# Joining a rewritten projection, held mamba weights and sums spread by products with the half-tile mamba kernel

## The chip, the cores and the metric

The kernel runs on one core of one Trainium2 chip. The metric is the device time of one execution in microseconds (us), as the median of several runs. The engines of a core work in parallel, each through its own list of instructions, and wait for one another by semaphores: PE (TensorE) multiplies matrices, DVE (VectorE), ACT (ScalarE) and POOL (GpSimd) work on elements, and SP (SyncE) here only issues transfers. POOL issues transfers too, on a queue of its own.

## The reference

One layer over x of 2 batches x 2048 tokens x 256 channels (T = 4096 rows), all in float32:

```python
xn = _layernorm(x)
x = x + mamba(xn, ...) + ffn(xn, ...)
# mamba: inner width 512, state 16, convolution over 4 taps, low rank 64
x_and_res = xn @ W_in; xs = silu(conv(x_and_res[:, :512]))
dt = softplus((xs @ W_x)[:, :64] @ W_dt + b_dt)
h_t = exp(dt*A) * h_(t-1) + dt*B*xs ; y = C.h + xs*D ; out = (y * silu(res)) @ W_out
# ffn: 16 heads of 16, then 8 experts of width 1024, one per token
hn = _layernorm(xn, g, b); q, k, v = hn @ wq + bq, hn @ wk + bk, hn @ wv + bv
x1 = xn + softmax(q k / 4) v @ wo + bo
hn2 = _layernorm(x1, g2, b2); idx = argmax(hn2 @ gate_w + gate_b)
result = x1 + relu(hn2 @ w1[idx] + b1[idx]) @ w2[idx] + b2[idx]
```

## The kernel before

The work runs in five stages, one after the other. Each stage is a block in which every engine has its own list, and the next block begins when all of them have ended. Rows are taken in 8 chunks of 512 tokens (`BANK`), four tiles of 128 rows each (`TG`).

**Projection** (`phase_project`, lines 112 to 430). A chunk of x is loaded by POOL (L201) into one of two buffers `X[s]`. DVE takes its moments (`variance`: bn_stats L379, bn_aggr L383, L385), ACT the root (L337), DVE refines it in five steps on tiny tiles (`rstd_steps`, L105 to L109) and normalises the rows in place (L392): that is xn, which SP stores to `xn_d` (L243). The same is done a second time on xn and gives `HN`, which POOL multiplies by g (L207) and adds b to (L211). PE turns both over (L301), ACT copies the turned xn out (L346) and DVE the turned HN (L422). PE then multiplies it for queries and keys (four products of 2 x 512 columns, L310) and for values (L316), with the value bias as one more product per tile (L318). ACT evicts each query or key tile twice (L353 in float32, L356 rounded to fp32r) and DVE forms the rest of the rounding (`QP[n][:, 1, :]`, L429), and SP stores both parts (L261). ACT copies the value tiles (L361) into one of two buffers, and SP stores each of four tiles per chunk (L266). The chunks run as a hardware loop over pairs; the normalisation of chunk c + 1 is laid between the query and key tiles of chunk c. POOL's order within chunk c is the scaling of chunk c + 1, then the load of chunk c + 2, which waits until PE has turned chunk c.

**Mamba** (`phase_mamba`). SP first loads ten weights (L879 to L888), among them `conv_w` copied to all partitions, and then the turned rows of the first two chunks (L891). DVE waits for all ten and makes the convolution weights of the four taps, eight products of 128x512 (`WC`, L1309). PE's first convolution (L1129) waits for them. The scans that follow are untouched by the change.

**Attention** (`phase_attention`). 32 items of one head group and one query block. PE makes the scores twice, once for their maxima (L642, reduced by DVE at L736) and once for the exponentials (L655, ACT at L714), and then the products with the values (L665). The maxima of an item reach the query tile as 16 small transfers (L574), for which the first L655 of the next item waits. At eight places, one in about four items, POOL loads three tiles of 512 KB for later (L623: xn, x and the output of mamba), adds the bias bo to the first (L625) and the mamba output to the second (L627).

**Routing** (`phase_route`). For each chunk SP loads the unscaled attention output into `OT` (L1438, four transfers) and the inverse row sums, each row copied to the 16 partitions of its head, into `SM` (L1446, four more). DVE multiplies them (`scale`, L1588), PE projects (L1513, into two buffers in turn), DVE adds the rows (L1592), takes moments and normalises (L1608), PE turns the rows over and makes gate logits (L1524, L1535), DVE chooses the expert and counts slots, POOL adds the base (L1490) and scatters the row numbers (L1495), SP stores `hn_d` and `base_d` (L1467, L1470). SP issues the loads of chunk c + 2 at the start of its turn c, behind the stores of chunk c - 1.

**Experts** (`phase_experts`). 23 tiles of 256 rows; untouched.

## Time and profile before

| what | us |
|---|---|
| median of 3 runs | 3401.77 (3387.27 to 3415.67) |
| the profiled execution | 3394.42 |
| span of its trace | 3392.8 |
| projection, from 0 to | 217.5 |
| mamba, to | 1320 |
| attention, to | 2865 |
| routing, to | 3040.3 |
| experts, to | 3392.8 |

The trace is of one execution. Its span leaves 1.6 us of the profiled time outside, and that execution is 7.4 us below the median.
### The profile page before, as it was taken

What the parts mean: (1) busy time and instruction counts of PE and PEld (TensorE: products, weight loads), DVE (VectorE), ACT (ScalarE), POOL (GpSimd) and SP (SyncE); (2) the same over time, 40 slices, a digit from 0 to 9 for tenths busy, and PEclk for the clock granted to TensorE, in tenths of its full rate; (3) what the DMA queues carried; (4) which work ended last, traced back from release to release, by engine and by line L of the source; (5) the groups of instructions that cost most, each with busy time, mean ns of one, the idle gap of its engine ahead of it and who ended that gap; (6) DMA issues with size and microseconds to landing.
All of it is one profiled execution on the core that took longest, in us unless ns stands there. A gap on an engine that the chain in (4) does not pass through costs nothing. (4 is left out here: it accounts for less than half of the span.)

```text
span 3392.8 us, 42834 instructions
## 1 busy us (share of the span) xinstructions
PE 2898.4 (85%) x12668; PEld 1374.2 (41%) x12668; DVE 2594.8 (76%) x3764; ACT 1708.7 (50%) x2088; POOL 930.6 (27%) x527
## 2 busy tenths in 40 slices
PE   5768799898998775999989999998999996539998
PEld 3333343343443332433333333333333332428887
DVE  5525999999999995988889888898989992542222
ACT  2324655655655631366667666676767776101110
POOL 2203565565565565000000000000000000234443
PEclk8879999999999887699999999999999998669999
DMA  4542122212121224655444555445554410336663
GB/s 150 170 141 81 64 75 81 69 75 80 69 84 66 69 68 55 78 86 68 68 76 62 85 68 80 74 60 79 67 86 60 63 21 27 112 106 198 200 204 120
DMA packets 218021, 300.80 MB, mean 89 GB/s; under 512 B 117906, under 2 KB 162476, under 8 KB 203346
## 3 DMA queue, kind: packets, MB, share of 16 engines
q1 hardware_dynamic: 205298, 268.27, 36.1%
q0 software_dynamic: 12512, 29.82, 2.9%
q8 instruction: 120, 1.97, 0.3%
q14 instruction: 91, 0.75, 0.1%
HBM read 245.37 MB, written 57.60 MB: 89 GB/s over the span
## 5 line engine op out<-in xcount | busy, mean ns | idle before, releaser
L736 DVE TENSOR_REDUCE attn_mx<-attn_pX 128x1 f32<-128x512 f32 x2048 | 1271.9, 683 | 187.8 <-PE attn_pX L642 185.9
L714 ACT ACTIVATE attn_pr<-attn_pS 128x1024 f32<-128x1024 f32 x1024 | 992.6, 1022 | 529.8 <-PE attn_pS L655 529.3
L642 PE MATMUL attn_pX<-attn_ks,attn_qs 48*128 48x512 f32 x2048 | 757.0, 497 | 75.0 <-DMA attn_vs<-v_d 25.2
L1198 PE MATMUL mamba_pY<-mamba_g,mamba_ident 128*128 128x512 f32 x1024 | 516.1, 651 | 139.9 <-DVE mamba_g L1351 139.7
L1331 DVE TENSOR_TENSOR_SCAN mamba_h<-mamba_pA,mamba_hs,mamba_db 128x512 f32<-128x512 f32 x512 | 616.7, 1263 | 12.9 <-ACT mamba_pA L1046 12.6
L642 PEld LDWEIGHTS attn_pX<-attn_ks,attn_qs 48*128 48x128 f32 x2048 | 308.3, 193 | 779.7 <-DVE attn_mx L736 715.5
L981 POOL TENSOR_TENSOR mamba_db<-mamba_bq,mamba_u 128x2048 f32<-128x2048 f32 x128 | 580.3, 4534 | 75.3 <-DVE mamba_u L1287 75.0
L665 PE MATMUL attn_pO<-attn_pr,attn_vs 128*17 128x512 f32 x4096 | 558.7, 618 | 0.4 <-ACT attn_pr L714 0.4
L1046 ACT ACTIVATE mamba_pA<-mamba_dt,mamba_an 128x512 f32<-128x512 f32 x512 | 352.7, 692 | 389.9 <-DVE mamba_h L1331 389.6
L655 PE MATMUL attn_pS<-attn_qs,attn_ks 50*128 50x512 f32 x2048 | 474.4, 418 | 52.9 <-DMA attn_qs<-attn_mt 32.7
L1198 PEld LDWEIGHTS mamba_pY<-mamba_g,mamba_ident 128*128 128x128 f32 x1024 | 200.9, 205 | 444.7 <-DVE mamba_g L1351 228.8
L1351 DVE TENSOR_TENSOR mamba_g<-mamba_h,mamba_bq 128x2048 f32<-128x2048 f32 x128 | 293.7, 2294 | 6.5
L655 PEld LDWEIGHTS attn_pS<-attn_qs,attn_ks 50*128 50x128 f32 x2048 | 258.4, 194 | 92.1 <-issue 55.1
L623 POOL DMA_DIRECT2D rows_xn<-xn_d x8 | 6.1, 767 | 1021.8 <-PE attn_pO L665 1021.8
L1129 PE MATMUL mamba_pP<-mamba_xt,mamba_wc 128*128 128x512 f32 x512 | 230.7, 596 | 24.2 <-DVE mamba_an L1312 24.2
L1875 DVE TENSOR_SCALAR exp_hm<-exp_pH,exp_b 128x256 f32<-128x256 f32 x46 | 22.3, 484 | 234.7 <-PE exp_pH L1813 234.7
L1839 ACT ACTIVATE exp_hm<-exp_pH,exp_b 128x256 f32<-128x256 f32 x46 | 21.8, 474 | 320.3 <-PE exp_pH L1813 320.3
L1813 PE MATMUL exp_pH<-exp_xt,exp_w 128*128 128x256 f32 x736 | 165.1, 383 | 1.1 <-DVE exp_xt L1854 1.1
L1826 PE MATMUL exp_pY<-exp_w,exp_hm 128*128 128x256 f32 x736 | 162.7, 379 | 0.0
L1129 PEld LDWEIGHTS mamba_pP<-mamba_xt,mamba_wc 128*128 128x128 f32 x512 | 97.7, 191 | 148.6 <-issue 148.6
L1813 PEld LDWEIGHTS exp_pH<-exp_xt,exp_w 128*128 128x128 f32 x736 | 141.4, 192 | 21.1 <-DVE exp_xt L1854 1.5
L1826 PEld LDWEIGHTS exp_pY<-exp_w,exp_hm 128*128 128x128 f32 x736 | 138.1, 190 | 17.9
(185 smaller groups left out, 1926.7 us busy)
## 6 DMA issues: line engine op xcount, KB each, us to landing
mamba_bq<-bc_d SPq DMA_DIRECT2D x64, 1024.0 KB, 4.6
attn_ks<-parts_d SPq DMA_DIRECT2D x192, 256.0 KB, 9.1
exp_w<-in_w SPq DMA_DIRECT2D x46, 1024.0 KB, 5.5
attn_vs<-v_d SPq DMA_DIRECT2D x32, 544.0 KB, 15.6
parts_d<-proj_qp SPq DMA_DIRECT2D x32, 512.0 KB, 2.9
attn_qs<-parts_d SPq DMA_DIRECT2D x192, 64.0 KB, 8.2
attn_qs<-attn_mt SPq DMA_DIRECT2D x512, 1.0 KB
oraw_d<-attn_oe SPq DMA_DIRECT2D x32, 256.0 KB, 2.1
```

Source lines behind the costliest of these rows:

```text
L642: pe.matmul(pX[bank(s, n)][:, :], QS[slot][rows, pair, qt * P:(qt + 1) * P], KS[slot][rows, pair, part * BANK:(part + 1) * BANK], start=Tr ...
L655: mm = pe.matmul(pS[pair][:, h, :], KS[slot][rows, pair, kt * P:(kt + 1) * P], QS[slot][rows, pair, :], start=True, stop=True)
L665: mm = pe.matmul(pO[32 * h:32 * h + VW, :], VS[s][:, kt, h, :], PR[2 * (kt % 2) + h // 2][:, h % 2, :], start=(kt == 0), stop=(kt == KT - 1))
L714: act.activation(PR[2 * (kt % 2) + pair][:, :, :], pS[pair][:, :, :], ACT.Exp, scale=HD ** -0.5).then_inc(p_sb, 1)
L736: dve.tensor_reduce(MX[:, col:col + 1], pX[bank(s, n)][:, :], AX.X, ALU.max).then_inc(x_max, 1)
L981: pool.tensor_tensor(DB[k % 2][:, :, :], BQ[q % 2][:, 0, :, :], U[s][:, j, :].unsqueeze(1).to_broadcast([P, QN, BANK]), ALU.mult).then_inc ...
L1046: act.activation(pA[n % 2][:, :], DT[s][:, j, :], ACT.Exp, scale=AN[:, j, q * QN + n:q * QN + n + 1]).then_inc(da_done, 1)
L1129: mm = pe.matmul(bank(par, place)[:, :], WC[:, k, a, w], XT[sx][:, k, a:a + BANK], start=(k == 0 and a == 0), stop=(k == KC - 1 and a == T ...
L1198: mm = pe.matmul(pY[j][:, :], ident[:, :], G[k % 2][:, n, :], start=False, stop=(q == NQ - 1 and n == QN - 1))
L1331: dve.tensor_tensor_scan(H[k % 2][:, n, :], pA[n % 2][:, :], DB[k % 2][:, n, :], HS[:, j, q * QN + n:q * QN + n + 1], ALU.mult, ALU.add).t ...
L1813: mm = pe.matmul(pH[n][:, f % 2, :], W1[s][:, k, f * P:(f + 1) * P], XT[s][:, k, :], start=(k == 0), stop=(k == KC - 1))
L1826: mm = pe.matmul(pY[s][:, t, :], HM[s][:, f, t * P:(t + 1) * P], W2[s][:, f, :], start=(f == 0), stop=(f == KF - 1))
```

## The change

The half-tile mamba kernel takes over three edits.

1. `phase_project` is written anew, with the eight chunks unrolled. Three buffers for x in place of two; the normalisation runs two chunks ahead in place of one; four buffers for the query and key parts in place of two; whole-chunk buffers for the values. xn is no longer stored to memory (`xn_d` is gone); its means and inverse roots are kept in `mv1` and `rstd1` instead. The product that added the value bias is gone; POOL adds it to a chunk of 128x1024 elements (`value_bias`).
2. The weights of mamba are loaded in the projection stage into tiles that are held through both stages, and POOL makes the tap products there, two in each of chunks 2 to 5. The mamba stage begins with the loads of its rows.
3. In attention POOL loads two tiles in place of three at each of the eight places and makes xn from x by a subtraction and a multiplication. In routing the inverse sums come as rows of 16 heads (`INV`, 7 small loads and the late ones), and PE spreads each to its 16 partitions by a product with a matrix of zeros and ones (`SEL`), two products of 512 columns per chunk; DVE multiplies from PSUM. `pA` is one buffer in place of two, and the loads of `OT` run three chunks ahead in place of two.

```diff
@@ phase_project, POOL
+                def value_bias(c):
+                    pool.wait_ge(v_sb, TG * (c + 1))
+                    v = VS[c % 2][:, :, :, 0:HD]
+                    pool.tensor_tensor(v, v, BV[:, :].rearrange("p (h d) -> p h d", d=HD).unsqueeze(1)
+                                       .to_broadcast([P, TG, HEADS, HD]), ALU.add).then_inc(v_done, 1)
+
+                for c in range(RX):
+                    load_x(c)
...
+                scale(0)
+                scale(1)
+                def tap(n):
+                    k, a = divmod(n, TAPS)
+                    a = TAPS - 1 - a
+                    pool.tensor_tensor(WC[:, k, a, :], WC[:, k, 0, :], CW[:, a, :], ALU.mult).then_inc(wc_done, 1)
+
+                for c in range(NCH):
+                    if c + RX < NCH:
+                        load_x(c + RX)
+                    value_bias(c)
+                    if c == 2:
+                        pool.wait_ge(mamba_ld, 16 * (len(mamba_w) + 1))
+                    if 2 <= c < 2 + KC * TAPS // 2:
+                        tap(2 * (c - 2))
+                        tap(2 * (c - 2) + 1)
+                    if c + 2 < NCH:
+                        scale(c + 2)
@@ SP
+                sp.dma_start(WC[:, :, 0, :], mamba_in[0]).then_inc(mamba_ld, 16)
+                for dst, src in zip(mamba_w[1:], mamba_in[1:]):
+                    sp.dma_start(dst, src).then_inc(mamba_ld, 16)
...
+                for c in range(NCH):
+                    store_turned(c)
+                    store_part(c, 0)
+                    store_part(c, 1)
+                    store_part(c, 2)
+                    store_part(c, 3)
+                    store_values(c)
+                sp.wait_ge(wc_done, KC * TAPS)
@@ PE
+                pe.wait_ge(id_ready, 2)
+                turn(0)
+                pe.wait_ge(w_in, 16 * 8)
+                for c in range(NCH):
+                    queries_keys(c)
+                    if c + 1 < NCH:
+                        turn(c + 1)
+                    values(c)
@@ ACT
+                for c in range(NCH):
+                    split(c, 0)
+                    split(c, 1)
+                    if c + 2 < NCH:
+                        root(c + 2, 0)
+                    split(c, 2)
+                    split(c, 3)
+                    if c + 1 < NCH:
+                        copy_turned(c + 1)
+                    if c + 2 < NCH:
+                        root(c + 2, 1)
+                    copy_values(c)
@@ DVE
+                for c in range(2):
+                    first_norm(c)
+                    second_norm(c)
+                    scaled_rows(c)
+                copy_turned(0)
+                for c in range(NCH):
+                    if c + 2 < NCH:
+                        first_norm(c + 2)
+                    low(c, 0)
+                    low(c, 1)
+                    if c + 2 < NCH:
+                        second_norm(c + 2)
+                    low(c, 2)
+                    low(c, 3)
+                    if c + 1 < NCH:
+                        copy_turned(c + 1)
+                    if c + 2 < NCH:
+                        scaled_rows(c + 2)
@@ phase_attention, POOL
-                    for dst, src in ((XN[c], xn_d), (XB[c], x), (MOB, mo_d)):
+                    for dst, src in ((XB[c], x), (MOB, mo_d)):
...
+                    pool.tensor_tensor(XN[c][:, :, :], XB[c][:, :, :], mean, ALU.subtract).then_inc(x_done, 1)
+                    pool.wait_ge(x_done, 3 * c + 1)
+                    pool.tensor_tensor(XN[c][:, :, :], XN[c][:, :, :], rstd, ALU.mult).then_inc(x_done, 1)
@@ phase_mamba
-                dve.wait_ge(w_ld, 16 * 10)
-                for a in range(TAPS - 1, -1, -1):
-                    for k in range(KC):
-                        ins = dve.tensor_tensor(WC[:, k, a, :], WC[:, k, 0, :], DB[0][:, a, :], ALU.mult)
-                ins.then_inc(ready_s, 1)
@@ phase_route, SP
+                for g in range(GB):
+                    load_inverses(0, g)
+                load_o(0)
+                for b in range(1, batches):
+                    for g in range(GB - (b == batches - 1)):
+                        load_inverses(b, g)
                 load_o(1)
-                load_r(1)
+                load_o(2)
@@ PE
+                def spread(c):
+                    if c >= 1:
+                        pe.wait_ge(scaled, c)
...
+                    for k in range(KC):
+                        mm = pe.matmul(pS[:, k, :], SEL[:, k, :], INV[:, c, :], start=True, stop=True)
+                    mm.then_inc(s_ps, 1)
...
                 for c in range(NCH):
                     if c + 1 < NCH:
                         project(c + 1)
+                    if c + 2 < NCH:
+                        spread(c + 2)
                     turn(c)
@@ DVE
-                    dve.tensor_tensor(OT[c][:, :, :], OT[c][:, :, :], SM[c][:, :, :], ALU.mult).then_inc(scaled, 1)
+                    dve.wait_ge(s_ps, c + 1)
+                    dve.tensor_tensor(OT[c][:, :, :], pS[:, :, :], OT[c][:, :, :], ALU.mult).then_inc(scaled, 1)
```

## Rows read from the trace of the kernel before

**Rows 1.** Busy time by stage: from:to, length, each engine (instructions), PEclk, DMA share, GB/s
```profile
0.00:217.50 217.50, 141.68 (x448) 76.32 (x448) 103.31 (x340) 64.05 (x129) 49.51 (x30) 0.88 0.51 161
...
1320.00:2865.00 1545.00, 1414.83 (x8194) 536.80 (x8192) 1301.82 (x2180) 1008.75 (x1058) 87.21 (x54) 0.94 0.48 68
2865.00:3040.30 175.30, 76.41 (x352) 65.02 (x352) 90.14 (x301) 18.38 (x41) 52.39 (x47) 0.65 0.35 99
```

**Rows 2.** The same view of seven projection periods and of seven routing periods
```profile
26.20:196.20 170.00, 124.06 (x393) 66.33 (x393) 88.01 (x284) 53.27 (x108) 42.36 (x20) 0.86 0.53 167
2888.60:3007.50 118.90, 59.95 (x284) 50.87 (x284) 69.27 (x227) 14.43 (x35) 37.14 (x27) 0.70 0.37 112
```

**Rows 3.** Who waited for whom in the projection: total us, times, longest
```profile
POOL proj_hn L207 <- DVE proj_hn L392: 141.8, 8, 19.9
DVE proj_stats L379 <- DMA proj_x<-in_x: 54.0, 7, 8.3
ACT proj_vs L361 <- DMA v_d<-proj_vs: 50.4, 16, 5.9
```

**Rows 4.** Timeline, projection: start, length, engine, line, operation, [idle before <-releaser]
```profile
20.86 2.34 POOL L211 TENSOR_TENSOR proj_hn<-proj_hn,proj_b 128x1024 f32<-128x1024 f32 x1
...
26.87 1.38 DVE L392 TENSOR_SCALAR proj_x<-proj_x,proj_meanvar,proj_rstd 128x256 f32<-128x256 f32 x4
...
31.34 0.69 DVE L429 TENSOR_TENSOR proj_qp<-proj_qf,proj_qp 128x512 fp32r<-128x512 f32 x1 [0.91 <-ACT proj_qp L356]
...
187.75 2.72 POOL L207 TENSOR_TENSOR proj_hn<-proj_hn,proj_g 128x1024 f32<-128x1024 f32 x1 [18.17 <-DVE proj_hn L392]
...
189.18 1.84 DVE L429 TENSOR_TENSOR proj_qp<-proj_qf,proj_qp 128x512 fp32r<-128x512 f32 x1 [0.91 <-ACT proj_qp L356]
...
209.77 0.69 PE L318 MATMUL proj_pV<-proj_bv,proj_one 1*128 1x256 f32 x2
```

**Rows 5.** Timeline, start of the mamba stage
```profile
217.55 0.39 SPq L879 DMA_DIRECT2D mamba_wc<-in_w_in  x1
...
229.67 4.91 DVE L1309 TENSOR_TENSOR mamba_wc<-mamba_wc,mamba_db 128x512 f32<-128x512 f32 x8 [11.46 <-DMA mamba_ds<-in_d_skip]
...
234.68 29.88 PE L1129 MATMUL mamba_pP<-mamba_xt,mamba_wc 128*128 128x512 f32 x64 [24.22 <-DVE mamba_an L1312]
```

**Rows 6.** Timeline of attention at one of the eight places
```profile
1768.59 0.77 POOL L623 DMA_DIRECT2D rows_xn<-xn_d  x1 [125.88 <-PE attn_pO L665]
...
1774.48 0.51 PE L655 MATMUL attn_pS<-attn_qs,attn_ks 50*128 50x512 f32 x2 [3.37 <-DMA attn_qs<-attn_mt]
```

**Rows 7.** Busy time in tens of us, attention, around two of the eight places
```profile
1760.00:1770.00 10.00, 9.72 (x59) 3.81 (x63) 9.39 (x16) 7.11 (x8) 1.41 (x2) 1.00 0.01 1
1770.00:1780.00 10.00, 4.88 (x26) 1.17 (x18) 4.80 (x8) 3.17 (x4) 3.97 (x4) 0.75 0.58 186
1780.00:1790.00 10.00, 9.50 (x50) 3.89 (x52) 6.26 (x10) 5.82 (x6) 1.53 (x1) 0.74 1.00 132
...
1910.00:1920.00 10.00, 8.15 (x43) 2.82 (x44) 6.50 (x11) 5.50 (x7) 4.73 (x4) 0.75 0.74 217
1920.00:1930.00 10.00, 9.75 (x56) 4.20 (x56) 8.59 (x14) 6.70 (x7) 1.29 (x1) 0.91 1.07 117
```

**Rows 8.** Instructions of line 736, attention: duration ns min/median/max
```profile
L736 DVE TENSOR_REDUCE attn_mx<-attn_pX x1992: 649/681/694, 1379.7 to 2814.1; 128x1 f32<-128x512 f32 x200
```

**Rows 9.** Waits, transfers (KB each) and one window of the routing stage
```profile
DVE route_ot L1588 <- DMA route_sm<-rs_d: 51.0, 6, 18.9
...
route_ot<-oraw_d SPq DMA_DIRECT2D x32, 128.0 KB
...
2874.00:2876.00 2.00, 0.00 (x0) 0.00 (x0) 0.00 (x0) 0.00 (x0) 0.00 (x0) 0.50 0.26 97
```

**Rows 10.** Timeline of the routing stage
```profile
2899.49 1.22 DVE L1592 TENSOR_TENSOR rows_xn<-route_pA,rows_xn 128x1024 f32<-128x1024 f32 x1 [3.77 <-PE route_pA L1513]
...
2917.69 4.23 DVE L1608 TENSOR_SCALAR route_hn<-rows_xn,route_meanvar,route_rstd 128x256 f32<-128x256 f32 x4
```

More of the change, by code:

```diff
@@ L161, in phase_project @@
         xn_done = m.sem("xn_done")
-        xn_out = [m.sem(f"xn_out{s}") for s in range(2)]
+        mamba_ld = m.sem("mamba_ld")
+        wc_done = m.sem("wc_done")
         hn_raw = m.sem("hn_raw")
@@ L363, in _, with root, copy_turned @@
-                chunks(act, body)
+                def root(c, n):
+                    act.wait_ge(var_ready, 2 * c + n + 1)
+                    act.activation(ROOT[:, :], V[:, :], ACT.Sqrt).then_inc(root_ready, 1)
+                def copy_turned(c):
+                    if c >= 2:
+                        act.wait_ge(xnT_out[c % 2], sum(pads(a) for a in range(c % 2, c, 2)))
+                    for k in range(KC):
+                        act.wait_ge(x_turned, KC * c + k + 1)
+                        act.copy(TX[c % 2][:, k, :], pT[k][:, :]).then_inc(x_sb, 1)
@@ new lines, in copy_values @@
+                def copy_values(c):
+                    if c >= 2:
+                        act.wait_ge(v_out[c % 2], 16 * GB * (c // 2))
+                    for t in range(TG):
+                        act.wait_ge(v_ps, TG * c + t + 1)
+                        act.copy(VS[c % 2][:, t, :, 0:HD], pV[t % 2][:, 0:C].rearrange("p (h d) -> p h d", d=HD)
+                                 ).then_inc(v_sb, 1)
+                for c in range(2):
+                    for n in range(2):
+                        root(c, n)
@@ L791, in phase_mamba @@
     NQ = N // QN
-    TAPS = conv_w.shape[0]
+    TAPS = WC.shape[2]
     PAD = TAPS - 1
@@ L1398, in phase_route @@
         CMP = m.sb("cmp", [P, NTL, NE])
-        pA = [m.ps(f"pA{n}", [P, TG, C]) for n in range(2)]
+        pA = m.ps("pA", [P, TG, C])
+        pS = m.ps("pS", [P, KC, BANK])
         pT = [m.ps(f"pT{n}", [P, 2, KC, P]) for n in range(2)]
```

491 lines of the change are left out of this document (229 added, 262 removed).

## The prediction

> **What bounds the kernel now.** I read the busy time by stage first [rows 1]. Attention is full: PE works 1414.8 of 1545 us. Projection and routing are not. In the projection no engine is busy for more than 142 of 217.5 us, and the DMA engines are at 0.51; in routing PE has 76 of 175 us and DVE 90. These two stages wait on chains, and the change works on them. Experts and the scans of mamba keep their instructions, so I take their time as it is.
>
> Then the waits of the projection [rows 3]. DVE waits 54.0 us in 7 of 8 chunks for the load of x, ACT 50.4 us for a value buffer to be stored, and POOL 141.8 us for rows to scale. That is one loop: POOL loads chunk c + 2 only after it has scaled chunk c + 1, so the load comes late, so DVE's moments, so the rows to scale. Seven periods, from the first chunk's first query product at 26.2 to the last chunk's, take 170 us, 24.3 each, in which DVE is busy 88.0 us (12.6 a period), PE 124.1 and POOL 42.4 [rows 2].
>
> Routing I read in the same way [rows 2, 9, 10]. Seven periods take 118.9 us, 17.0 each, though the first, to the next L1592 at 2899.5, takes 10.9. DVE waits 51.0 us for the `SM` loads. While only the `OT` and `SM` loads run, the DMA share is 0.26 at 97 GB/s. Eight loads of 128 KB (1.05 MB) thus take 10.7 us of every period.
>
> **Projection.** The new order removes the loop: x is loaded three ahead and the moments are two chunks ahead, so none of the three waits of [rows 3] is left to last. What bounds it next is DVE with POOL. DVE keeps its instructions, 12.6 us a chunk. POOL, which had two products of 2.34 us alone [rows 4], gets `value_bias` of the same size, 7.0 us in all, and in chunks 2 to 5 two taps of a quarter of that size each way, near 1.2 us each: 9.4 us.
>
> The rows show that these two don't simply lie side by side. L429 takes 1.84 us when it starts at 189.18 under L207, which runs from 187.75 for 2.72 us; the difference from its usual 0.69 is about the time that POOL still had [rows 4]. In routing four L1608 take 4.23 us under POOL [rows 10]. They have the elements of L392, four of which cost 1.38 us [rows 4], so 2.8 us were lost. L736, with one input in PSUM, never takes over 694 ns [rows 8], whatever POOL does. So DVE instructions that read SBUF wait for a POOL instruction under way, and others pass. About 4.9 of DVE's 12.6 us are such others (bn_stats, bn_aggr, copies from PSUM). The period is bounded by 14.4 us (12.6 and 1.8 for handing over between PE, ACT and DVE) if nothing collides, and by 12.6 + 7.0 = 19.6, or 22.0 with taps, if all does. I lay one period out: the scaling product runs beside the next moments, but then holds the first `low`, and `value_bias` holds the last one. That gives 17.8 us, and 20 with taps, nearer the upper bound, since both groups of `low` come just when POOL has something ready.
>
> The Trainium skill (SBUF — State Buffer, Who interferes with whom) says the same more sharply, and it speaks against moving work to POOL: the pair is an exclusive lock that one instruction holds for its whole length, `tensor_tensor` contends when both inputs lie in SBUF, and `tensor_reduce` never does. By that rule, the trace agrees (1.84 us against 0.69).
>
> PE is no bound: its 124.1 us in seven periods are 17.7 each at a clock of 0.86, and the bias products (0.69 us per tile in [rows 4]) fall away, some 2.8 us. The transfers are none either: 0.53 of 24.3 us is 12.9 us a chunk, of 4.1 MB, less an eighth for xn.
>
> The start gets longer. DVE now does two chunks before the first copy for PE, and the second one's normalisation waits for POOL's product that ends at 23.2 [rows 4]. I put the first query product at 32 (before: 26.2). Then two periods of 17.8, four of 20, chunk 6 without new rows at 12.4 (PE's products and turning at the upper clock), and chunk 7 at 10.3: 32 + 35.6 + 80 + 12.4 + 10.3 = 170.3. The tail was 7 us (last value product 210.5, stage end 217.5); it gets `value_bias` in the chain, so 9. The stage ends at 179 in place of 217.5: **38 us saved**. With 14.4 us throughout it would end near 150 (67 saved), with 19.6 and 22.0 near 191 (26 saved). The 3 MB of weights and taps lie in the first 20 us of the queue, where stores have nothing to do yet; if they delayed the third x by some us, it is inside these bounds.
>
> **Mamba start.** From the first load at 217.55 to PE's first convolution there are 17.1 us: 12 for weights to land, 4.9 for the taps [rows 5]. What remains is the load of the first rows, 515 KB, for which I take 4 us (the twelve of before moved some 3.5 MB; half a MB is under 2, and as much for issue and landing). **13 us saved**, with 11 and 14 as ends. PE idles before in both cases, so its first convolutions are at the lower clock in both.
>
> **Attention.** At each of eight places 1.5 MB of loads from POOL fall on the 16 small transfers of the maxima. PE waits (3.37 us in [rows 6]), and its clock then goes from 1.00 to 0.50 for a while. PE issued 76 products in the 20 us after 1770, where undisturbed it issues 60 in ten, and 99 after 1910 [rows 7]: 7 and 3.5 us lost, so some 5 a place and 42 in all. One third of the bytes goes. I take a little less than a third of it, **12 us saved**; below is 0 (the small transfers still end behind the other two loads), above 30 (the clock isn't lost at most places). The two added POOL products, 4.7 us a place, hide behind L736, which doesn't wait for POOL [rows 8]. If that cover were gone, they would cost 8 x 4.7 = 38 us.
>
> **Routing.** The `SM` loads go, half of the 10.7 us. 17.0 - 5.3 = 11.7 is then what the transfers need. DVE is busy 69.3/7 = 9.9 us a period; the fastest period seen is 10.9 [rows 10]. PE gets two products of 512 columns per chunk, 1.7 us at the upper clock and 3.4 at the lower, beside DVE's normalising, but now behind one `pA`. I take 12.3: 118.9 - 86.1 = **33 us saved**. The bounds are 10.9 (43 saved) and 15 (14 saved), where PE at its lower clock sets it: 60 us of PE in seven periods at 0.70 [rows 2] make 12 each at 0.50, and 3.4 more. The first `SM` gives way to seven small loads in front of `scale(0)` and a product; I take that start as even.
>
> **The sum.** 38 + 13 + 12 + 33 = 96. The profiled execution of before took 3394.4, so 3298. It is 7 us below the median of 3401.8, which would give 3306; I say 3300.
>
> **Rivals.**
> - *POOL doesn't hold DVE in the new order* (periods of 14.4): for it, only some of the products of the rows are held; against it, `low` and the scaling are both due once a chunk. 29 us more saved: 3271.
> - *Routing isn't helped*, since PE at the lower clock, with one `pA` and the spreading in its chain, takes 15.4 to 16 us a period: for it PEclk 0.65 in the stage [rows 1]. 26 us less saved: 3326.
> - *Attention keeps its clock* at most places, since a shorter stall might not cost it: 20 more saved, 3280. Against it, the smaller disturbance at 1910 lost the clock too (0.75, [rows 7]).
> - *No change or slower.* One mechanism could do it: in the projection POOL's list (load, bias, taps, scaling) becomes the loop that everything waits for, each link in turn, as it was with the loads. It decides when the projection's mean period passes 33 us (24.3 now, and 58 us of gains elsewhere over seven periods). POOL, DVE and PE's longest shares, one after the other, are 9.4 + 12.6 + 10 = 32. So even a full chain gives about 3395, no change. Three chunks of buffers speak against it.
> - *The change doesn't do what it says*: the taps or weights end the projection late, since SP waits for them. Taps are done in chunk 5, two periods before the end, so I give it nothing of its own.
>
> **How the numbers follow.** Forecast as summed 0.57 (its own range 3280 to 3318), POOL harmless 0.14, attention keeps its clock 0.10, routing not helped 0.14, chain in the projection 0.05. From 3255 (the first and third together) to 3340 (routing not helped and 19.6 us periods) leaves out 2 in 10. About 1%, 34 us, is what a measurement of this kernel can tell from no change. Every case but the last is faster by more; half of the last and a little of the routing case with other losses fall inside: faster 0.94, same 0.04, slower 0.02.
>
> **What would show it.** Right: no wait of DVE for x; L429 and the normalising over their lone times under POOL; PE's first convolution 4 us after the stage's first load; waits for the maxima at eight places, shorter; no wait of `scale` for loads in routing. Wrong: projection periods under 15 or over 22 us; L736 over 694 ns; routing periods at 15.

## The result and the profile after

| | kernel before | changed kernel |
|---|---|---|
| median | 3396.34 us (3387.27 to 3415.67, 4 runs) | 3313.62 us (3312.34 to 3314.77, 4 runs) |
| ratio, with its 95% interval | 1 | 0.9749 (0.9704 to 0.9794) |
| span of the profiled execution | 3392.8 | 3310.9 |
| projection | 217.5 | 174.3 |
| mamba, first load to first convolution | 17.1 | 3.7 |
| mamba, the rest | 1089.0 | 1088.2 |
| attention | 1543.4 | 1551.6 |
| routing | 173.3 | 140.1 |
| experts | 352.5 | 353.0 |

The changed kernel is faster by 2.5%, 82 us. Stages are read from the first instruction of one to the first of the next (so the end of mamba before is 1323.6 and that of attention 2867.0, where the rows above had the rounder 1320 and 2865). They say where the 82 us come from: 43.2 from the projection, 13.5 from the start of mamba, 33.2 from routing, 1 from mamba's rest. Attention gave 8.2 back.

The stages of the changed kernel (the view of busy time by stretch; columns as in [rows 1]: from:to, length, PE, PE loads, DVE, ACT, POOL, granted clock, DMA share, GB/s). The last two rows answer to [rows 2]: the seven periods of the projection and of routing.

```profile
0.00:174.30 174.30, 113.58 (x384) 69.58 (x384) 135.45 (x339) 63.45 (x129) 74.60 (x46) 0.92 0.72 195
...
1266.20:2817.80 1551.60, 1421.73 (x8192) 538.15 (x8192) 1300.53 (x2180) 1008.34 (x1058) 111.57 (x63) 0.93 0.47 65
2817.80:2957.90 140.10, 95.70 (x384) 72.02 (x384) 95.19 (x301) 17.89 (x41) 52.36 (x51) 0.68 0.50 93
```

```profile
31.00:152.80 121.80, 99.08 (x337) 60.68 (x338) 112.16 (x258) 53.58 (x109) 61.13 (x33) 0.92 0.73 196
2841.20:2925.40 84.20, 75.30 (x312) 56.50 (x312) 74.32 (x227) 13.52 (x34) 36.11 (x27) 0.78 0.64 113
```

Seven executions with this same projection ended it between 172.4 and 176.4 us, so differences of 4 us between two of them mean nothing. DVE is now busy for 112.2 of 121.8 us, where it was 88.0 of 170. It has fewer instructions there than in [rows 2] (258 for 284, since two chunks are normalised before the first period) and takes more time for them: it waits inside its instructions. In routing DVE is busy for 74.3 of 84.2 us. Two of the seven periods take 10.8 and 10.9 us, the other five 12.5 or 12.6. Each of those five holds one tiny DVE instruction that took 2.90 to 2.95 us for its usual 0.17 or 0.19, beside POOL's addition of the rows (L1506); the two short periods hold none:

```profile
2884.20 2.90 DVE L1653 TENSOR_TENSOR route_oh<-route_wtt,route_mw 128x32 f32<-128x32 f32 x1
2884.69 2.35 POOL L1506 TENSOR_TENSOR rows_xb<-rows_xb,rows_xn 128x1024 f32<-128x1024 f32 x1
```

So DVE, held by POOL once a period, bounds the five: in four of them, read one by one, it is busy for 11.7 or 11.8 of 12.5 us, and the period is the same whether the clock is 0.73 or 0.86. PE isn't far behind (10.8 to 12.2 us busy), and no run shows what the period would be without the hold. In the kernel before, the same instruction (L1621) took 0.19 us in all eight chunks, and three others were held in seven periods (two L1608 of 3.26 us, one L107 of 2.94).

The timeline of the projection (start, length, engine, line, operation; lines between are left out):

```profile
68.82 3.43 DVE L437 TENSOR_TENSOR proj_qp<-proj_qf,proj_qp 128x512 fp32r<-128x512 f32 x2
...
68.96 2.74 POOL L198 TENSOR_TENSOR proj_hn<-proj_hn,proj_b 128x1024 f32<-128x1024 f32 x1
...
135.82 5.25 DVE L411 TENSOR_SCALAR proj_hn<-proj_x,proj_meanvar,proj_rstd 128x256 f32<-128x256 f32 x4
135.87 2.17 POOL L204 TENSOR_TENSOR proj_vs<-proj_vs,proj_bv 128x1024 f32<-128x1024 f32 x1 [8.26 <-ACT proj_vs L365]
138.00 2.60 POOL L216 TENSOR_TENSOR held_wc<-held_wc,proj_cw 128x512 f32<-128x512 f32 x2
```

The pair of low parts (L437) takes 3.43 us under the scaling (L198), where two take 1.29 alone. The normalising of chunk 7 (L411) takes 5.25 for 1.38 us, and ends at 141.1, half a us after bias and taps.

The start of mamba, which answers to [rows 5]:

```profile
174.32 0.89 SPq L903 DMA_DIRECT2D mamba_xt<-xnT_d  x2
...
177.99 29.50 PE L1140 MATMUL mamba_pP<-mamba_xt,held_wc 128*128 128x512 f32 x64 [14.60 <-DMA mamba_xt<-xnT_d]
```

One of the eight places in attention, which answers to [rows 6]: SP issues the 16 small transfers of the maxima, one every 0.68 us, POOL issues its two loads before SP is through, and PE waits.

```profile
2128.59 10.88 SPq L600 DMA_DIRECT2D attn_qs<-attn_mt  x16
...
2137.86 0.78 POOL L649 DMA_DIRECT2D rows_xb<-in_x  x1 [130.96 <-PE attn_pO L697]
2138.63 0.76 POOL L649 DMA_DIRECT2D attn_mob<-mo_d  x1
...
2143.03 0.50 PE L687 MATMUL attn_pS<-attn_qs,attn_ks 50*128 50x512 f32 x2 [2.63 <-DMA attn_qs<-attn_mt]
```

The last small transfer is issued from 2138.84 to 2139.5, just after the issue of the second load has begun. In the whole stage PE's wait for them is what it was (32.7 us before; waits: total, times, longest):

```profile
PE attn_pS L687 <- DMA attn_qs<-attn_mt: 32.5, 26, 4.5
```

The clock is lost at the places as it was ([rows 7]; here around 1992):

```profile
1992.20:2002.20 10.00, 6.51 (x34) 2.16 (x32) 4.91 (x8) 4.40 (x5) 5.29 (x4) 0.76 0.33 106
2002.20:2012.20 10.00, 9.93 (x54) 4.18 (x51) 7.58 (x13) 5.88 (x7) 4.69 (x2) 0.73 0.94 137
2012.20:2022.20 10.00, 9.65 (x62) 3.39 (x58) 9.39 (x16) 7.64 (x8) 0.00 (x0) 1.00 1.06 117
```

In routing DVE itself no longer waits for loads ([rows 9]); what it waits for is the first spreading, for which PE in turn waits 15.5 us until the inverse sums have landed, and three of the projections:

```profile
DVE route_ot L1620 <- PE route_pS L1531: 15.1, 1, 15.1
...
DVE rows_xn L1624 <- PE route_pA L1540: 8.9, 3, 3.8
```

### The profile page after: what moved, and what is told of

Same layout as the page of the kernel before. It is cut to its first block and busy times, and to the rows that moved or that the text cites. A ratio compares the mean times of both kernels' runs of the same rounds, so it can differ in the third digit from the quotient of the medians.

```text
span 3310.9 us, 42346 instructions
## 1 busy us (share of the span) xinstructions
PE 2899.2 (88%) x12636; PEld 1377.2 (42%) x12636; DVE 2625.1 (79%) x3755; ACT 1707.4 (52%) x2088; POOL 979.1 (30%) x554
## 5 line engine op out<-in xcount | busy, mean ns | idle before, releaser
L768 DVE TENSOR_REDUCE attn_mx<-attn_pX 128x1 f32<-128x512 f32 x2048 | 1271.3, 683 | 197.6 <-PE attn_pX L674 197.5
L1057 ACT ACTIVATE mamba_pA<-mamba_dt,held_an 128x512 f32<-128x512 f32 x512 | 352.6, 692 | 390.2 <-DVE mamba_h L1335 389.8
L687 PE MATMUL attn_pS<-attn_qs,attn_ks 50*128 50x512 f32 x2048 | 478.2, 421 | 52.8 <-DMA attn_qs<-attn_mt 32.5
L1140 PE MATMUL mamba_pP<-mamba_xt,held_wc 128*128 128x512 f32 x512 | 230.3, 596 | 14.6 <-DMA mamba_xt<-xnT_d 14.6
L1140 PEld LDWEIGHTS mamba_pP<-mamba_xt,held_wc 128*128 128x128 f32 x512 | 97.5, 191 | 139.0 <-issue 124.0
## 6 DMA issues: line engine op xcount, KB each, us to landing
attn_vs<-v_d SPq DMA_DIRECT2D x32, 544.0 KB, 15.7
```

What stands on the lines that cost most here:

```text
L687: mm = pe.matmul(pS[pair][:, h, :], KS[slot][rows, pair, kt * P:(kt + 1) * P], QS[slot][rows, pair, :], start=True, stop=True)
L768: dve.tensor_reduce(MX[:, col:col + 1], pX[bank(s, n)][:, :], AX.X, ALU.max).then_inc(x_max, 1)
L1057: act.activation(pA[n % 2][:, :], DT[s][:, j, :], ACT.Exp, scale=AN[:, j, q * QN + n:q * QN + n + 1]).then_inc(da_done, 1)
L1140: mm = pe.matmul(bank(par, place)[:, :], WC[:, k, a, w], XT[sx][:, k, a:a + BANK], start=(k == 0 and a == 0), stop=(k == KC - 1 and a == T ...
```

## The experiments

Each run has a short name, given behind "Measured" and used in the table of attention. "Unchanged" is the changed kernel as it came. A second comparison of it ("again") had a profiled execution with a span of 3306.0 us, and a median of 3319.73 (ratio 0.9779, 0.9756 to 0.9802), so two medians of one kernel lie 6 us apart. The medians of the kernel before, measured anew in each comparison, lie between 3394.0 and 3403.8; a ratio compares kernels of different comparisons better than a median does. A stage's time is that of one profiled execution.

### Attention: other moments for POOL's loads

First, the loads half an item earlier:

```diff
-                    pool.wait_ge(pv_done, (3 * c + 2) * KT)
+                    pool.wait_ge(pv_done, (3 * c + 2) * KT - KT // 2)
```

> The changed kernel, with POOL's two loads at each of the eight places in attention issued half an item earlier (about 22 us), clear of the 16 small transfers of the maxima. Only the order moves, nothing is left out. Theory A (the stall comes from the small transfers that are issued last and lie behind 1 MB of POOL's load; a third fewer bytes doesn't end it, another time does): PE waits no longer for attn_qs at the places, the granted clock stays at 1.00 there, and attention falls from 1551.6 us by 5 a place, to about 1512. Rival B (the stall belongs to the maxima's own transfers, which SP needs 10.9 us to issue, and happens with or without the load): attention stays within 5 us of 1551. Rival C (the loads lower the clock wherever they fall): the low clock moves with the loads, no gain.

Measured ("shift"): median 3307.85 us (3296.99 to 3328.05), ratio 0.972 (0.969 to 0.975). In its profile attention took 1563.9 us. That execution was the slowest of the four, 20 us over the median, and the median lies below the two of the unchanged kernel, so 1563.9 overstates what the edit cost. Its attention fits none of the theories, but its places show what happened:

```profile
1418.20 1.89 POOL L655 TENSOR_TENSOR rows_xn<-rows_xn,norm_rstd 128x1024 f32<-128x1024 f32 x1
1418.20 1.92 DVE L778 TENSOR_TENSOR attn_ms<-attn_mn,attn_ms 128x16 fp32r<-128x16 f32 x1
```

```profile
1416.00:1426.00 10.00, 7.89 (x38) 3.35 (x39) 7.84 (x14) 3.88 (x4) 8.46 (x4) 0.74 0.01 1
1426.00:1436.00 10.00, 10.00 (x46) 3.78 (x42) 6.70 (x12) 5.41 (x6) 0.00 (x0) 0.57 0.01 3
```

The products moved with the loads, onto the small DVE operations that split the maxima. L778, 0.17 us long, took 1.92, exactly to the end of POOL's product, the next maxima came late, and PE waited 2.03 us for them. The clock fell with no transfer under way (DMA share 0.01). PE's wait for the maxima at the places is gone (11.9 us in the whole stage for 32.5), as theory A says of the loads. What is lost by the clock at the places is as much as with the loads (27 us for 22, in the table below), but now beside the products.

Then the products were put back, behind a second wait:

```diff
                     pool.wait_ge(x_in, 32 * (c + 1))
+                    pool.wait_ge(pv_done, (3 * c + 2) * KT)
```

> The changed kernel, with POOL's two loads at each of the eight places in attention issued half an item earlier (as in the run before), but POOL's four products held back to their old moment. The first shift put the products onto DVE's small operations that split the maxima (L775 to L785), whose rows grew from 0.17 to 1.92 us. Theory A (the small transfers issued last lie behind POOL's load; and the products, where they are, cost nothing): with the loads away and the products back, PE doesn't wait for attn_qs at the places, the granted clock stays at 1.00 there, and attention falls to 1505 to 1525 us (1543 to 1554 in four executions of the unchanged code). Rival B (the transfers of the maxima come too late by themselves): attention stays at 1543 to 1554 with the wait for attn_qs at 30 us.

Measured ("shift2"): median 3293.24 us (3290.58 to 3299.0), ratio 0.9676 (0.9659 to 0.9693): 20 to 26 us below the changed kernel's two medians, 25 to 35 us by the ratios. Attention took 1527.0 us, just above the range of theory A. Around the place that was shown above the clock is kept:

```profile
1960.65 0.78 POOL L649 DMA_DIRECT2D rows_xb<-in_x  x1 [105.87 <-PE attn_pO L698]
...
1982.48 1.89 POOL L654 TENSOR_TENSOR rows_xn<-rows_xb,norm_meanvar 128x1024 f32<-128x1024 f32 x1 [20.30 <-PE attn_pO L698]
```

```profile
1980.80:1990.80 10.00, 9.62 (x61) 3.77 (x63) 9.20 (x15) 7.64 (x9) 8.15 (x4) 1.00 0.11 32
1990.80:2000.80 10.00, 9.67 (x62) 3.57 (x60) 9.35 (x16) 7.46 (x8) 0.34 (x1) 1.00 1.02 127
```

```profile
PE attn_pS L688 <- DMA attn_qs<-attn_mt: 13.6, 24, 4.5
```

POOL works for 8.15 of the ten us from 1980.8 and DVE and PE lose nothing, so the four products, at this moment, cost nothing that shows. PE issues 123 products in 20 us, where the changed kernel had 88. The wait fell from 32.5 to 13.6 us. The stall was thus made by the loads lying in front of the last small transfers.

### Attention: the third load back

```diff
-                    for dst, src in ((XB[c], x), (MOB, mo_d)):
+                    for dst, src in ((XN[c], x), (XB[c], x), (MOB, mo_d)):
```

> The changed kernel, with a third load of 512 KB at each of the eight places (x into the tile of xn, which the subtraction then overwrites), so the transfers are those of the kernel before and the two added products stay. Theory A (the stall's length doesn't follow the bytes, once the small transfers are behind any load): attention within 6 us of 1551.6. My recorded theory (5 us a place, a third of it by the third load): about 12 us longer, 1564.

Measured ("three"): median 3321.8 us (3316.49 to 3330.82), ratio 0.9772 (0.9739 to 0.9804), attention 1561.0 us, PE's wait for the maxima 35.9 us against 32.5. The median is 8 us above the first and 2 above the second median of the unchanged kernel, so it doesn't part the theories. PE's wait grew by 3.4 us in all, and 1.8 of that lie at one place. What the clock loses at the places is in the next table.

This run doesn't test what more bytes in front of the small transfers cost, because the third load isn't in front of them. It is issued 1.5 us after the first one, and the last small transfer goes out 0.7 to 1.0 us after it. So the third load is behind the last small transfer at seven places of this run, and at all sixteen of the kernel before's two executions. At the one place where it was in front, PE waited 5.25 us. Counted over the 88 places of eleven executions (all in the table below but "shift", "shift2" and "best"), the wait goes with the loads that were issued ahead of the last small transfer:

| loads of 512 KB ahead | places | PE's wait, us | mean |
|---|---|---|---|
| one | 26 | 1.78 to 2.83 | 2.04 |
| two | 61 | 2.63 to 4.21 | 3.20 |
| three | 1 | 5.25 | 5.25 |

That is a count and not an experiment: the places with one load ahead are also those at which POOL's first load comes a little later. But it agrees with a wait that grows by some 1.2 us for each load in front, and it says why cutting the third one gained nothing.

### Attention: what an execution loses by its clock

> The changed kernel once more, unchanged, for a second profile. Attention took 1551.6 us in the first, and 1543.6 to 1562.0 in five executions of kernels with the same attention. Theory A (attention is 1482 us of work, the same to 4 us in every profile, and what the granted clock loses in episodes whose length differs from execution to execution): the stage less the lost time is 1478 to 1487 again, and the lost time is anywhere from 60 to 85. Rival B (the changed attention is 8 us slower than that of before by its own work): the stage less the lost time is the same too, but 8 us over that of the kernel before.

> The kernel before once more, unchanged, for a second profile. Attention took 1543.4 us in the first, of which 59.1 are lost by a lower clock. Theory A (the lost time is chance in its length, and it was low in the first profile; three loads or two at a place make no difference): attention less the lost time is 1484 within 4, and the lost time is anywhere from 59 to 85. Rival B (before loses less than the changed kernel by its nature): again 59 to 62.

To tell chance from cause I took from each profile the granted clock in stretches of 5 us, from 60 us after the start of attention to 60 us before its end, and summed 5 x (1 - clock). "Places" are six of the eight; the other two lie within 25 us of the end of a loop iteration, where PE pauses for 2.8 to 3.6 us in both kernels. "Iterations" are the four ends of an iteration that are clear of a place. Whether an episode counts to one or the other is sure to about 1 us. In "shift" the places are those where the products run now. All in us:

```
kernel          attention   lost   attention - lost   places   iterations
before            1543.4    59.1        1484.3          22.7      13.1
before2           1536.7    47.1        1489.6          15.3       8.5
unchanged         1551.6    71.0        1480.6          17.1      23.8
again             1550.4    62.2        1488.1          17.1      22.7
pebias            1543.6    62.6        1481.0          23.9      11.9
ahead2            1553.6    67.4        1486.2          22.2      18.9
tapsdve           1562.0    83.5        1478.5          18.8      35.4
nobias            1561.5    81.6        1479.9          24.5      30.0
vdve              1554.9    67.6        1487.2          34.1      11.9
routesm           1551.0    67.5        1483.5          18.9      24.0
three             1561.0    76.2        1484.8          21.4      28.1
shift             1563.9    89.6        1474.3          27.3      25.6
shift2            1527.0    48.6        1478.3           0.0      20.5
best              1524.1    45.5        1478.6           0.8      24.8
```

The rows from "unchanged" to "routesm" are eight executions with the same instructions in attention. Three things follow. First, attention less its lost time is 1478 to 1490 us in every row but "shift" (1474): its own work didn't change. Theory A of both runs holds in that but for 1 to 2 us ("again" 1488.1 for at most 1487, "before2" 1489.6 for at most 1488). Second, two loads or three make no difference at the places: 22 us are lost in the mean of the eight, 19 in the two of before, 21 with the third load back. As the count above shows, two loads at most lay in front in all of these but one place. With the loads out of the way it is 0 and 1. Third, the lost time may be more than chance: before loses 47 and 59 us, the eight lose 62 to 84, and of the difference (17 us in the means) 11 lie at the four clear ends of an iteration, which the change doesn't touch. So the part of theory A by which the lost time of before would be 59 to 85 fell, and so did its rival (59 to 62), though two executions of before are few. But it isn't a property of the changed attention: "pebias" and "vdve", whose attention has the same instructions, lose 11.9 there, as before does (13.1 and 8.5). The traces show a companion of it. In "before", "before2" and "pebias" PE pauses once at each of these ends. In the other eleven executions it mostly pauses a second time some 6 us later, for 0.8 to 3.5 us. Whether the second pause keeps the clock down or the low clock makes the pause isn't shown, nor is what sets it off. The third load back leaves it as it is. The two added products lie elsewhere, but a kernel without them wasn't tried.

### Projection: the value bias on PE again

```diff
+                        mm = pe.matmul(pV[t % 2][:, 0:C], ONE[:, :], BV[:, :], start=False, stop=True)
...
-                    value_bias(c)
```

> The changed kernel, with the value bias as a product on PE again, as in the kernel before, and POOL's addition gone from the projection. Theory A (DVE instructions that read SBUF wait for a POOL instruction under way, and POOL's 2.2 us of bias come just under the last low part): periods of 16.8 us fall by about 2, those of 18.8 with taps by about 2 too, the tail by 2.2, and the stage ends near 157 in place of 174.3. Rival B (PE's chain sets the period: the bias products at 0.35 us a tile go onto it): periods as they are or 1 us longer, only the tail gains; the stage ends at 170 to 176.

Measured ("pebias"): median 3304.14 us (3299.95 to 3308.46), ratio 0.9716 (0.969 to 0.9742), but the stage ends at 176.0, at the upper end of what the unchanged projection takes. Rival B is right about the stage. The lower median comes from elsewhere, in the profile from attention (1543.6), and its cause is open, as said above. From the first to the last query product:

```profile
30.01:154.00 123.99, 120.35 (x392) 65.43 (x392) 91.23 (x258) 53.44 (x109) 46.12 (x27) 0.92 0.78 193
```

PE is busy for 120.4 of 124.0 us, and DVE falls from 112.2 to 91.2. Both sides of the trade show: POOL's 2.2 us a chunk had cost DVE 21 us in seven periods, and the same bias costs PE 3.0 us a chunk (120.4 for 99.1 us in seven), which makes PE the bound.

### Projection: taps by DVE at its end

```diff
-                    if 2 <= c < 2 + KC * TAPS // 2:
-                        tap(2 * (c - 2))
-                        tap(2 * (c - 2) + 1)
...
+                for k in range(KC):
+                    for a in range(TAPS - 1, -1, -1):
+                        dve.tensor_tensor(WC[:, k, a, :], WC[:, k, 0, :], CW[:, a, :], ALU.mult).then_inc(wc_done, 1)
```

> The changed kernel, with the eight tap products made by DVE at the end of its list in the projection, where it waits for nothing but the end of the stage, and not by POOL in chunks 2 to 5. Theory A (POOL's taps hold DVE: the periods of chunks 3 to 5 are 18.8, 18.5 and 18.9 us, those without taps 16.8; the scaled rows of chunk 7 take 5.25 for 1.38 us under bias and taps): every period is 16.8 or under, and the stage ends 7 to 11 us earlier, near 165. Rival B (taps lie in POOL's idle time and cost nothing): the stage ends at 174 as it does, or later by DVE's 4.9 us.

Measured ("tapsdve"): the stage ends at 168.3, 6.0 us earlier (4 to 8 earlier than the seven executions of the unchanged projection). That is theory A in kind, with less than its 7 to 11 us. Periods, from the starts of the first query products, are 15.2, 16.8, 16.8, 18.2, 16.9, 16.9 and 13.0, against 14.4, 16.8, 16.8, 18.8, 18.5, 18.9 and 17.5. So each pair of taps costs 0.6 to 2.0 us in its period, and the last pair costs 4.5 us in chunk 6. The periods give 7.9 us. The start is 1.1 us earlier, but no tap has run by then, and it varies from 29.2 to 31.0 without a change. The stage's end gains less, since the tail from the last value product grew from 10.9 to 14.0 us: the last four stores of the values take 5.8 to 8.7 us to land, for 4.0 to 6.0. Why isn't shown. The taps, of which the first meets POOL's last bias, take 6.87 us on DVE and end at 159.6, so they don't set the end. The median, 3319.51 us (ratio 0.9764, 0.974 to 0.9788), doesn't show the 6 us; attention took 1562.0 in its profile.

### Projection: no value bias at all

> The changed kernel without the value bias: POOL's addition is left out and nobody makes it, so v lacks its bias; the stores of the values wait for the copies. With the product on PE the stage didn't get shorter (176.0 against 174.3), since PE took 2.8 us a chunk. Theory A (POOL's bias holds DVE for 2.2 us a period, and PE's chain took its place as the bound): with nobody making it, the periods fall by 1.5 to 2.5 us each, and the stage ends at 155 to 160. Rival B (the period is bounded by PE, ACT and DVE handing over, not by POOL): periods within 0.5 us of 14.4 to 18.8 as they are, the stage ends near 172, by the tail alone.

Measured ("nobias"): the stage ends at 165.2, 9.1 us earlier, between the two theories. Periods are 15.1, 15.7, 18.4, 17.7, 17.7, 15.3 and 12.5: those with taps, though they have no bias beside them, are still near 18. The seven sum to 112.3 for 121.7. So POOL's bias costs 9.4 us over the periods, 1.3 each. Part of the rest is PE waiting for ACT to take value tiles (15.1 us in five waits, 6.0 in three with the bias), behind a root for which ACT waits for DVE's moments (13.7 us). There is one execution, of 3316.48 us.

### Projection: the bias by DVE out of PSUM

```diff
+                    dve.tensor_tensor(VS[c % 2][:, t, :, 0:HD], pV[t % 2][:, 0:C].rearrange("p (h d) -> p h d", d=HD),
+                                      BV[:, :].rearrange("p (h d) -> p h d", d=HD), ALU.add).then_inc(v_sb, 1)
```

> The changed kernel, with the taps by DVE at the end as in the run beside it, and the value bias added by DVE while it takes the value tiles out of PSUM (which ACT did before): POOL is left with the scaling alone, and nothing is left out. Theory A (POOL's products cost twice, their own time and what they hold of DVE): though DVE gets four instructions of some 0.4 us a chunk more, periods fall to 15 or 16, the stage ends near 155 to 162. Rival B (DVE is the bound by its own work, and more of it makes it slower): periods of 17 to 18.5, the stage ends at 170 to 180.

Measured ("vdve"): the stage ends at 163.0, 11.3 us earlier; median 3310.79 us (3302.92 to 3314.97), ratio 0.9724 (0.9701 to 0.9747). The seven periods:

```profile
30.54:142.19 111.65, 95.29 (x337) 58.61 (x338) 94.21 (x285) 43.72 (x82) 35.24 (x19) 0.94 0.85 211
```

DVE has 27 instructions more in this stretch than in the changed kernel, and is busy for 18 us less. Periods are 15.9 us in the mean for 17.4. That is theory A, with an end 1 us beyond its range: DVE's own instructions cost it less than POOL's bias and taps did. The new addition reads one of its inputs in PSUM: it took 0.41 to 0.43 us both alone (20 times) and beside a POOL product (12 times).

### Routing: two chunks ahead

```diff
-    AHEAD = 3
+    AHEAD = 2
```

> The changed kernel, with the loads of OT two chunks ahead in routing, as before, and not three. Theory A (the period fell because half the bytes are gone, and DVE with POOL is the bound at 12.5 us): seven periods stay at 84 us and the stage within 3 us of 140.1. Rival B (the third buffer ahead did it, since SP issues a load behind two waits for stores): DVE waits for the loads of OT, periods near 14 to 15, the stage 10 to 17 us longer.

Measured ("ahead2"): median 3329.27 us (3328.96 to 3329.6), ratio 0.9794 (0.9769 to 0.982), the stage 153.9 us. Periods are 10.3, 12.5, 12.6, 12.5, 26.5, 12.6 and 12.5. Neither theory: six periods are as short as with three ahead, and DVE waits 14.9 us for one chunk's loads.

```profile
DVE route_ot L1619 <- DMA route_ot<-oraw_d: 14.9, 1, 14.9
```

```profile
2894.38 13.74 SPq L1447 DMA_DIRECT2D route_ot<-oraw_d  x4
...
2915.16 3.39 SPq L1447 DMA_DIRECT2D route_ot<-oraw_d  x4
```

SP needed 13.74 us to issue four loads that take 3.4 elsewhere; why isn't known. The third chunk ahead hides such a delay: over the ten executions with it (and without the loads of the next run) the stage took 139.5 to 147.6 us.

### Routing: the removed transfers back

The spreading by products stays; four loads of 128 KB a chunk, of which nobody reads the result, are added. The scaling waits for them all the same, since they count in the same semaphore (`O_IN` is 8 transfers in place of 4):

```diff
+                            sp.dma_start(SM[c % RING][half, k, :], rs_d[i * GH:(i + 1) * GH, :].unsqueeze(1)
+                                         .to_broadcast([GH, HD, BANK])).then_inc(o_in[c % RING], 16)
```

> The changed kernel, to which the transfers that the change took out of routing are given back: for each chunk four loads of 128 KB of inverse sums into tiles that nobody reads, in the order of the kernel before, while the spreading by products stays. Theory A (the period fell because half of the bytes ahead of the scaling went): DVE waits for OT again, periods go back to 15 to 17 us, the stage is 20 to 33 us longer than 140.1. Rival B (it fell because the loads run three chunks ahead and not two): periods stay near 12.5, the stage at 140 to 150.

Measured ("routesm"): median 3344.92 us (3342.75 to 3347.33), ratio 0.9852 (0.9828 to 0.9875), 25 us over the unchanged kernel in the same comparison; the stage 169.4 us, periods 15.5 in the mean. DVE waits for the loads again:

```profile
DVE route_ot L1634 <- DMA route_sm<-rs_d: 26.9, 4, 12.8
```

That is theory A: the removed transfers are worth 29 us of the stage even with three chunks ahead (22 to 30 against the ten executions). Whether by their bytes or by the time that SP takes to issue four more isn't parted.

### The three gains together

The edits of "shift2", "tapsdve" and "vdve" in one kernel.

> The changed kernel with three edits of the runs before together: POOL's loads in attention half an item earlier with the products where they were, taps by DVE at the end of the projection, and the value bias by DVE on the way out of PSUM. If the gains stand side by side, as they lie in different stages: 3293 of the earlier loads alone, less 11 us of the projection (163.0 against 174.3), makes 3280 to 3286. If the projection's gain is lost again by what the clock does later: 3293.

Measured ("best"): median 3263.16 us (3258.95 to 3275.45, 5 runs), ratio 0.9603 (0.9584 to 0.9623). That is 131 us below the kernel before and 57 below the unchanged kernel in the same comparison. The projection ends at 161.6, attention takes 1524.1. It is 17 us faster than the lower end of what was expected; the profiled execution was the slowest of the five (3275.45), so where the other four found the rest isn't in a trace.

## Why the prediction was right, and where it wasn't

The total was right, with two terms off in opposite directions, projection by +5 and attention by -20. Against the sum of 96, 82 us came, and the median of 3313.6 lies inside the range of 3280 to 3318.

**Projection: right, 43 for 38.** That DVE is held by POOL instructions under way is what the trace shows, and the experiments on POOL's list give it its price. As the prediction put it, "DVE instructions that read SBUF wait", it is too wide: bn_stats (L400) reads SBUF and took 0.41 us in the 28 cases beside a POOL product as in the 36 alone, which the prediction's own list of exceptions had. The start was 31.0 for 32. The two plain periods of 17.8 were 14.4 and 16.8; those that I put at 20 were 16.8, 18.8, 18.5 and 18.9. The list of taps begins one period later than I laid it out, behind the value bias of chunk 2 at the end of that chunk's period. For the same reason the step "chunk 6 without new rows at 12.4" was wrong: it took 17.5, because the bias and the taps of chunk 5 fell on the normalising of chunk 7. With the taps away it was 13.0. The tail, with the bias in its chain, was 10.9 for 9. So the 5 us by which the sum is off are 12 us less in the start and the periods and 7 us more in chunk 6 and the tail: that it came so near is in part luck.

**Start of mamba: right.** 3.7 us for 4.

**Attention: the step that failed, 8 lost for 12 saved.** It read: "One third of the bytes goes. I take a little less than a third of it". The bound below, 0 since "the small transfers still end behind the other two loads", was the case. The step before it was already wrong: "1.5 MB of loads from POOL fall on the 16 small transfers". I hadn't set the moments of the two beside each other, though the trace of before has them:

```profile
1759.34 10.88 SPq L574 DMA_DIRECT2D attn_qs<-attn_mt  x16
...
1770.09 0.75 POOL L623 DMA_DIRECT2D attn_mob<-mo_d  x1
```

SP begins its last small transfer at 1769.6. POOL's first two loads are issued at 1768.6 and 1769.35, the third at 1770.1. So 1 MB at most lay in front of a small transfer and the third load behind all of them, there and at the other seven places. Taking one load out moved the other two up and left as much in front as before: PE's wait for the maxima stayed at 32.5 us for 32.7. I had priced a place at 5 us, from two places. With the loads elsewhere attention was 27 us shorter than the mean of the eight (1527.0 against 1553.6), 22 of it lost clock: 3.3 a place. The wait for the maxima fell by 19 us as well, of which only 5 show in attention less its lost time. The 8 us by which attention got longer are not from the places: 17 us are lost there for 23. They lie at the ends of the iterations, for which no run has shown a cause, and two kernels with the same attention don't have them.

The cover of the two added products held (L768 took 681 ns in the median as before; its 700 at most is 6 ns over the 694 that I had set as a sign of being wrong, and nothing follows from that), but only by their moment: moved by half an item they cost the clock as much as the loads.

**Routing: right in the amount, 33 for 33, with some luck.** The period of 12.3 was 12.0. Its reason was only a part: the removed transfers are worth 22 to 30 us, and the third chunk ahead, for which I had no term, 6 to 14 (153.9 against 139.5 to 147.6), by covering a late transfer. The two overlap, and the start of the stage, which I took as even, got 2 us longer. And it isn't transfers that bound the period now, as I had it (11.7), but DVE, at 12.5 in five of seven, with one tiny instruction a period held for 2.7 us by POOL. I knew the holding and used it in the projection, but not here. What the single `pA` costs wasn't tried; DVE waits for it 8.9 us in all.

**Rivals.** "POOL harmless": only the first period had its 14.4. "Routing not helped" and "chain in the projection" didn't come. "Attention keeps its clock" didn't come with the change. Moving the loads does it, and gave 20 to 26 us where I had written 20 for the change.

**The signs.** Of those for right, the waits for the maxima weren't shorter. Of those for wrong, one projection period of seven was under 15 (14.4); the other two didn't come, but for the 6 ns named above.

## What to carry to other kernels

A collision between transfers is priced by what is issued ahead of the short, urgent one, and not by all the bytes that move around it. Look at the moment at which it is issued, and move the long ones before cutting one that lies behind. Work given to POOL costs twice where DVE runs a `tensor_tensor` on two SBUF inputs or a `tensor_scalar` at that moment, however small, and nothing where DVE takes statistics or reads PSUM; put it there, and move only the transfers when the transfers are the trouble. Where a stage is 1480 us of work and 45 to 90 of lost clock, split the two before any difference under 1% is explained.

## What the runs showed of the hardware

- **A tiny DVE instruction can wait as long as a large one.** L778, 128x16 elements, took 0.17 us in the median of its 32 and 2.2 at most, under a POOL product of 1.89 to 2.38 us ("shift"). The Trainium skill (SBUF — State Buffer, Who interferes with whom) says that the loser of the shared pair fully blocks; the trace agrees.
- **Which forms are held.** In the changed kernel's projection, beside POOL: `tensor_tensor` on two SBUF inputs (L437) up to 2.84 us for 0.69, `tensor_scalar` (L411) up to 2.37 for 0.41 and on 128x4 elements (L405) up to 1.92 for 0.17. As alone: bn_stats (L400, 0.41), the copy from PSUM (L432, 0.68), the reduction from PSUM in attention (L768, 0.70 at most), and a `tensor_tensor` with one input in PSUM ("vdve", 0.43 at most).
- **POOL's instruction gets longer too.** L198 took 2.74 us with DVE's low parts beside it and 2.34 in "vdve". In the case shown above a low part was under way when L198 began; whether L198 waited for it or ran slower isn't shown.
- **A transfer's issue can take long.** Four issues on SP took 3.4 us in most chunks and 13.74 in one ("ahead2"), in which SP issued nothing else.
- **Small transfers behind large ones on another queue.** 16 transfers of 1 KB came 1.78 to 2.83 us late for PE with one load of 512 KB issued ahead of the last of them, 2.63 to 4.21 with two.
- **The clock at a stall.** A stall of PE of 1.0 us left the granted clock at 1.00 (the first place with the loads moved). Stalls of 2.6 to 3.4 us lowered it to 0.50, the level of 1.2 GHz, for a part of the next 20 us, at one place for a short time and at the next for a long one, in the same kernel. Of stalls of 1.9 to 2.0 us, both of the changed kernel's first profile lowered it and both of its second didn't.
